# A convolution with a gated low-rank layer: the first five tiles in another order, and the router's query turned by VectorE

## What is computed

```python
out = conv1d(x, weight, groups=4, pad=4) + (c @ c_weight.T)[:, :, None] + bias[None, :, None]   # (32, 64, 1024)
q = einsum('bsd,rd->bsr', out, Wq_w)                  # router query, 16 numbers a row
scores = einsum('bsr,er->bse', q, keys)               # 64 experts
gate = softmax over the 16 best scores, 0 elsewhere
z = einsum('bsd,nd->bsn', out, A_w)                   # 512 = 64 experts x 8
y = einsum('bsn,on->bso', z * gate per expert, B_w) * 2.0
result = x + y                                        # fp32
```

## Time and profile before

| | |
|---|---|
| median of 3 runs | 237.67 us (236.91 to 238.66) |
| profiled execution, own time | 237.78 us |
| span in the profile | 235.8 us |
| granted TensorE clock, mean | 1.0 |
| TensorE busy | 231.0 us of the span |
| VectorE busy | 179.2 us |
| ScalarE busy | 98.3 us |
| HBM traffic | 161 GB/s over the span |

### The profile page before, as it was taken

The page is one execution under the profiler, slowest core; times in us unless marked ns, Lnnn a source line. Parts: engine busy times, 40 slices in busy tenths (PEclk is TensorE's granted clock), DMA queues, the critical chain, the costliest instruction groups (busy, mean ns, idle before and its releaser), DMA issues.

```text
span 235.8 us, 3992 instructions
## 1 busy us (share of the span) xinstructions
PE 231.0 (98%) x1398; PEld 206.4 (88%) x1398; DVE 179.2 (76%) x421; ACT 98.3 (42%) x245; POOL 1.6 (1%) x9
## 2 busy tenths in 40 slices
PE   8999999899999999999999999999999999999995
PEld 8988998598988989898898989889898988989884
DVE  1797799999969697996979698796969865644522
ACT  3897866255353253525424352532426241202100
POOL 2000000000000000000000000000000000000000
PEclk9999999999999999999999999999999999999999
DMA  6999017384644628263462816347282432616222
GB/s 196 379 403 379 10 47 224 100 276 161 177 152 100 244 70 258 77 186 147 105 235 71 276 58 194 138 105 234 72 240 93 121 146 51 220 45 222 92 89 89
DMA packets 22915, 38.22 MB, mean 162 GB/s; under 512 B 2544, under 2 KB 11120, under 8 KB 22896
## 3 DMA queue, kind: packets, MB, share of 16 engines
q1 hardware_dynamic: 22752, 37.89, 49.4%
q10 hardware_dynamic: 144, 0.08, 0.2%
HBM read 25.64 MB, written 12.32 MB: 161 GB/s over the span
## 4 chain that ended last, share of the span: by engine, by line
PE 93%; DVE 3%; issue 3%; ACT 0%; POOL 0%; DVEq 0%; POOLq 0%
PE p_z L608 36%; PE p_out L652 12%; PE p_out L653 12%; PE p_out L660 12%; PE p_conv L564 10%; PE p_conv L516 4%; PE p_out L608 3%; PE p_t L669 2%; PE p_out L516 1%; PE p_t L673 1%; DVE z_g L848 1%; PE p_t L622 1%; DVE h_lo L726 0%; DVE h_t L771 0%; DVE zt_lo L726 0%
## 5 line engine op out<-in xcount | busy, mean ns | idle before, releaser
L652 PE MATMUL p_out<-b_hi,zt_hi 128*128 128x512 f32 (+1 forms) x128 | 50.2, 393 | 0.0
L653 PE MATMUL p_out<-b_hi,zt_lo 128*128 128x512 f32 (+1 forms) x128 | 50.1, 393 | 0.0
L608 PE MATMUL p_z<-a_hi,h_hi 128*128 128x264 f32 x240 | 34.1, 285 | 1.0 <-DVE z_g L848 1.0
L608 PE MATMUL p_z<-a_lo,h_hi 128*128 128x264 f32 x240 | 35.0, 289 | 0.0
L660 PE MATMUL p_out<-b_lo,zt_hi 128*128 128x512 f32 (+1 forms) x128 | 34.5, 392 | 0.0
L608 PEld LDWEIGHTS p_z<-a_hi,h_hi 128*128 128x128 f32 x240 | 32.0, 188 | 2.6 <-issue 1.4
L608 PE MATMUL p_z<-a_hi,h_lo 128*128 128x264 f32 x240 | 34.2, 285 | 0.0
L608 PEld LDWEIGHTS p_z<-a_hi,h_lo 128*128 128x128 f32 x240 | 31.3, 188 | 0.0
L608 PEld LDWEIGHTS p_z<-a_lo,h_hi 128*128 128x128 f32 x240 | 31.0, 188 | 0.0
L343 ACT ACTIVATE h_hi<-h_t 128x1024 fp32r<-128x1024 f32 x16 | 17.0, 1064 | 31.5 <-DVE h_t L771 31.5
L726 DVE TENSOR_TENSOR x_lo<-x_blk,x_hi 128x1536 fp32r<-128x1536 f32 (+4 forms) x18 | 25.5, 1419 | 6.1 <-ACT x_hi L343 5.9
(11 more groups left out here) (100 smaller groups left out, 259.1 us busy)
## 6 DMA issues: line engine op xcount, KB each, us to landing
x_nat<-in_x_rows SPq DMA_DIRECT2D x16, 512.0 KB, 5.0
out_dram<-x_nat SPq DMA_DIRECT2D x31, 256.0 KB, 2.8
x_blk<-in_x_blocks SPq DMA_DIRECT2D x14, 516.0 KB, 4.4
z_dram<-a_raw SPq DMA_DIRECT2D x60, 64.0 KB, 1.8
a_raw<-z_dram SPq DMA_DIRECT2D x15, 256.0 KB, 3.8
a_raw<-in_a_wq SPq DMA_DIRECT2D x8, 264.0 KB, 6.3
x_nat<-in_b_w SPq DMA_DIRECT2D x4, 512.0 KB, 9.2
x_blk<-in_x_blocks SPq DMA_DIRECT2D x2, 258.0 KB, 3.9
```

The source lines that it names most:

```text
L608: mm = nc.tensor.matmul(z_bank(t, b)[:, 0:HB], h[:, t % 2, r, :], a[:, r, b * HB:(b + 1) * HB], start=k == 0 and r == 0, stop=k == 2 and r ...
L652: nc.tensor.matmul(dst, zt_hi[:, t % 2, c, :], b_hi[:, c, cols], start=c == 0, stop=False)
L653: nc.tensor.matmul(dst, zt_lo[:, t % 2, c, :], b_hi[:, c, cols], start=False, stop=False)
```

## The change

In the steady loop, from tile 5 on (TS = 5), TensorE no longer turns the query. ScalarE writes it twice side by side into `q_s` (128 rows by 32), VectorE turns it in four blocks of 32 by 32 into the diagonal blocks of `q_d`, ScalarE rounds that to `q_hi`, and one VectorE instruction makes `q_t`: its rows hold the high part and, under a mask column, the low part. The keys get a second set of 64 columns, so `scores` has 128 columns, and a sum over the two halves takes the place of the copy of the scores. TensorE's body becomes: z of tile i, the three shared products of the convolution of tile i+2 (`conv_sum`), `scores(i)`, the other six (`conv_pair`), and the second product. Tiles 3 and 4 take the way of tiles 0 to 2.

In the beginning, one of the eight products of ones goes, `cw` and the products for `u` are made in two halves (`products_u(0)` ahead of `conv_first`, `products_u(1)` behind its first four matmuls), and the lists of ScalarE and VectorE are in another order. On SP's queue, `z_in(1)` moves ahead of `load_rows(1)`. `small` grows from 164 to 229 columns.

```diff
 TW = 5
-TS = 3
+TS = 5
 NN = 8
...
-        q_s = sb("q_s", [P, P], F32R)
+        q_w = sb("q_w", [P, P])
+        q_s = sb("q_s", [P, 2 * RD])
+        q_d = sb("q_d", [P, P])
+        q_hi = sb("q_hi", [P, P], F32R)
         q_f = sb("q_f", [P, P])
         q_t = sb("q_t", [P, P], F32R)
-        k_r = sb("k_r", [P, E], F32R)
+        k_r = sb("k_r", [P, 2 * E], F32R)
+        k_hi = sb("k_hi", [P, E], F32R)
         sc = sb("sc", [P, E])
...
             z_out(1)
+            z_in(1)
             load_rows(1)
-            z_in(1)
             load_rows(2)
...
             nc.gpsimd.memset(ident[:], 0.0).then_inc(s_iz, 1)
-            nc.gpsimd.memset(q_s[:].bitcast(F32), 0.0).then_inc(s_qz, 1)
+            nc.gpsimd.memset(q_w[:], 0.0).then_inc(s_qz, 1)
+            nc.gpsimd.memset(q_d[:], 0.0).then_inc(s_qdz, 1)
             pool.wait_ge(s_iz, 1)
...
                                     pattern=[[-1, P]], channel_multiplier=1).then_inc(s_ident, 1)
-            pool.wait_ge(s_small, 16)
-            nc.gpsimd.tensor_copy(cw[:], sm[:, SMALL_CW:SMALL_CW + 64].rearrange("d (g c) -> d g c", c=CI).unsqueeze(2)
-                                  .to_broadcast([P, NG, R, CI])).then_inc(s_cw, 1)
+            pool.wait_ge(s_cw, 1)
+            nc.gpsimd.tensor_copy(cw[:, 2:NG], sm[:, SMALL_CW + 2 * CI:SMALL_CW + NG * CI].rearrange("d (g c) -> d g c", c=CI)
+                                  .unsqueeze(2).to_broadcast([P, NG - 2, R, CI])).then_inc(s_cw, 1)
...
                 act.wait_ge(s_cs, t - TW + 1)
+                if t == 2 * TG:
+                    act.wait_ge(s_u, 2)
                 if t > TW:
...
                     act.wait_ge(s_qz, 1)
-                if i >= 1:
+                if 1 <= i < TS:
                     act.wait_ge(s_qtp, i)
+                if i > TS:
+                    act.wait_ge(s_qd, i - TS)
                 query = z_bank(i, 1)[:, J - HB:HB]
                 if i < TS:
-                    high(q_s[:, 0:RD].bitcast(F32), query, s_q)
+                    high(q_w[:, 0:RD], query, s_q)
                 else:
-                    high(q_s[:, 0:4 * RD].rearrange("p (k d) -> p k d", d=2 * RD)[:, :, 0:RD],
-                         query.unsqueeze(1).to_broadcast([P, 2, RD]), s_q)
+                    high(q_s[:].rearrange("t (k d) -> t k d", k=2), query.unsqueeze(1).to_broadcast([P, 2, RD]), s_q)
...
                 act.wait_ge(s_qtp, i + 1)
-                high(q_f[:] if i < TS else q_t[:], p_t[:, 0:P], s_qt)
+                high(q_f[:], p_t[:, 0:P], s_qt)
+            def split_q(i):
+                act.wait_ge(s_qd, i - TS + 1)
+                high(q_hi[:], q_d[:], s_qhi)
...
                 act.wait_ge(s_small, 16)
-                high(k_r[:], sm[:, SMALL_K:SMALL_K + E], s_khi)
+                high(k_r[:, 0:E], sm[:, SMALL_K:SMALL_K + E], s_khi)
+                high(k_hi[:], sm[:, SMALL_KH:SMALL_KH + E], s_khi)
...
             take_q(0)
+            split_h(1)
             copy_q(0)
-            split_h(1)
             add_u(3)
-            split_x(4)
-            split_w(1)
             exp(0)
             split_h(2)
+            split_x(4)
+            take_q(1)
+            split_w(1)
+            copy_q(1)
             split_b(0)
             split_b(1)
-            take_q(1)
-            copy_q(1)
+            take_q(2)
+            exp(1)
+            copy_q(2)
+            split_h(3)
+            split_z(0)
             split_b(2)
-            exp(1)
-            take_q(2)
-            split_h(3)
-            copy_q(2)
             split_b(3)
-            split_z(0)
             add_u(4)
+            exp(2)
             sum_w(1)
-            exp(2)
             split_x(5)
             take_q(3)
+            split_z(1)
             split_h(4)
-            split_z(1)
             for i in range(3, NT):
...
                     take_q(i)
-                copy_q(i)
+                if i < TS:
+                    copy_q(i)
+                else:
+                    split_q(i)
                 if i > 3:
...
+            def products_u(pair):
+                pe.wait_ge(s_cw, pair + 1)
+                for g in (2 * pair, 2 * pair + 1):
+                    mm = nc.tensor.matmul(u_bank(pair)[:, g % 2 * P:g % 2 * P + SMALL_KH - SMALL_C], cw[:, g].rearrange("d r c -> d (r c)"),
+                                          sm[:, SMALL_C:SMALL_KH], start=True, stop=True)
+                mm.then_inc(s_up, 1)
...
                     direct(0, 0, ab, 0, True, False)
+                products_u(1)
                 pe.wait_ge(*x_lo_done(0, 0))
...
-            def conv_shared(t):
+            def conv_sum(t):
                 g = t // TG
...
+            def conv_pair(t):
+                g = t // TG
                 for ab in range(2):
...
             def conv(t):
-                if t >= TW:
-                    conv_shared(t)
-                else:
-                    conv_direct(t, (0, 2, 1))
+                conv_direct(t, (0, 2, 1))
...
                         pe.wait_ge(s_hhi, t + 1)
+                        if t == 0:
+                            pe.wait_ge(s_u, 2)
                         if t == 1:
...
                 pe.wait_ge(s_q, i + 1)
-                if i >= TS:
-                    pe.wait_ge(s_qlo, i - TS + 1)
                 if i == 0:
...
                     pe.wait_ge(s_qt, i)
-                nc.tensor.transpose(p_t[:, 0:P], q_s[:].bitcast(F32), ident[:]).then_inc(s_qtp, 1)
+                nc.tensor.transpose(p_t[:, 0:P], q_w[:], ident[:]).then_inc(s_qtp, 1)
...
             def scores(i):
-                pe.wait_ge(s_qt, i + 1)
+                if i < TS:
+                    pe.wait_ge(s_qt, i + 1)
+                else:
+                    pe.wait_ge(s_qlo, i - TS + 1)
                 if i == TS:
...
             pe.wait_ge(s_ones, 1)
-            for _ in range(8):
+            for _ in range(7):
                 nc.tensor.matmul(p_t[:, 0:P], ones[:], ones[:], start=True, stop=True)
-            pe.wait_ge(s_cw, 1)
-            for g in range(NG):
-                mm = nc.tensor.matmul(p_t[:, g * P:g * P + SMALL - SMALL_C],
-                                      cw[:, g].rearrange("d r c -> d (r c)"),
-                                      sm[:, SMALL_C:SMALL], start=True, stop=True)
-            mm.then_inc(s_up, 1)
+            products_u(0)
             conv_first()
...
                 z_product(i, 1, (0,), range(R))
-                turn_q(i)
+                if i < TS:
+                    turn_q(i)
                 z_product(i, 2, (0,), range(R))
+                if i + 2 < NT:
+                    conv_sum(i + 2)
                 scores(i)
                 if i + 2 < NT:
-                    conv(i + 2)
+                    conv_pair(i + 2)
                 out_part(i - 2, 0)
...
             def split_keys():
-                dve.wait_ge(s_khi, 1)
-                low(k_r[2 * RD:3 * RD], sm[2 * RD:3 * RD, SMALL_K:SMALL_K + E], k_r[2 * RD:3 * RD], s_klo)
+                dve.wait_ge(s_khi, 2)
+                low(k_r[:, E:2 * E], sm[:, SMALL_KH:SMALL_KH + E], k_hi[:], s_klo)
+            def turn_q(i):
+                dve.wait_ge(s_q, i + 1)
+                if i == TS:
+                    dve.wait_ge(s_qdz, 1)
+                for b in range(4):
+                    block = slice(32 * b, 32 * b + 32)
+                    last = nc.vector.transpose(q_d[block, block], q_s[block, :])
+                last.then_inc(s_qd, 1)
             def split_q(i):
-                dve.wait_ge(s_q, i + 1)
-                low(q_s[:, RD:2 * RD], z_bank(i, 1)[:, J - HB:HB], q_s[:, 0:RD], s_qlo)
+                dve.wait_ge(s_qhi, i - TS + 1)
+                dve.wait_ge(s_scp, i)
+                nc.vector.scalar_tensor_tensor(out=q_t[:], in0=q_hi[:].bitcast(F32), scalar=sm[:, SMALL_M:SMALL_M + 1],
+                                               in1=q_d[:], op0=ALU.mult, op1=ALU.add).then_inc(s_qlo, 1)
...
                 dve.wait_ge(s_scp, i + 1)
-                nc.vector.tensor_copy(sc[:], scores_at(i)).then_inc(s_dve, 1)
+                scored = scores_at(i)
+                if i < TS:
+                    nc.vector.tensor_copy(sc[:], scored).then_inc(s_dve, 1)
+                else:
+                    nc.vector.tensor_reduce(sc[:], scored.rearrange("t (k e) -> t e k", k=2), axis=mybir.AxisListType.X,
+                                            op=ALU.add).then_inc(s_dve, 1)
...
+            def add_bias(pair):
+                gs = slice(2 * pair, 2 * pair + 2)
+                dve.wait_ge(s_up, pair + 1)
+                nc.vector.tensor_tensor(u[:, gs], u_bank(pair)[:, 0:2 * P].rearrange("c (g n) -> c g n", n=P)[:, :, 0:32],
+                                        sm[:, SMALL_B + 2 * pair:SMALL_B + 2 * pair + 2].unsqueeze(2).to_broadcast([P, 2, 32]),
+                                        ALU.add).then_inc(s_u, 1)
+            dve.wait_ge(s_small, 16)
```

(60 more changed lines are left out.)

## The result

The changed kernel runs in 235.5 us (median of 6, 235.1 to 235.88) against 238.06 for the kernel before on the same chip: 0.9912 of it, interval 0.9886 to 0.9938. In a second set it was 235.26 against 237.6: 0.9903, interval 0.9875 to 0.9931. The forecast was 235.4.

The account below looks back on a forecast made before the run. TensorE's own list was taken to bound the kernel, with VectorE setting the time in the beginning. From the profiled 237.78 us, -1.29 (beginning), -1.32 (turn) and +0.22 (fp32 scores) gave 235.39, forecast 235.4, range 234.7 to 237.0.

Parts of the forecast that it names:

- The beginning: Tiles 0 to 4: VectorE's list between the copy for tile 1 and tile 2's gate shrinks, tile 3 starts earlier, -1.29 us.
- The pause for the exponential: VectorE's wait before tile 2's weighing: 0.44 us saved, since exp(2) now stands ahead of sum_w(1) on ScalarE.
- My ceiling of 1.55: Start of tile 3: TensorE's own work would allow 45.05 us, so at most 1.55 us could be gained.
- The turn: TensorE's list, tiles 5 to 15: the query's turn leaves it, 0.12 us a tile, -1.32 over eleven tiles.
- keep their price: Scores among TensorE's convolution products: 0.11 us for 64 columns and for 128, bounded by a weight load.
- The price of 56 to 81 ns: Lower price per turn from the skill: 0.6 to 0.9 us for eleven turns, a time of 235.9 to 236.1.
- fp32 scores: Tiles 3 and 4 on TensorE: two instructions for one, 0.11 us more each, +0.22.
- The first 20 us: Start of the kernel, one product of ones less and u's products moved: next to nothing, 0 to -0.1 us, not counted.
- The new wait: scores(i) waits for VectorE's split_q: 2.3 us of work fits in 3.18, 0.8 left, about 0.1 in tile 14.
- the deciding point: VectorE's query blocks: from 0.40 us a block the new way exceeds its cover; each further 0.1 costs 0.4 a tile.
- Rival (D): Slower: the query's new way is longer than its cover; 239.8 us at 0.5 us a block; chance 0.08.
- VectorE's load: Steady tiles: VectorE's work grows by 1.1 us a tile, first MAX8 0.28 later, the gate's wait stays covered.

Follow-up runs that it names:

- the doses: Changed kernel with each of the four query blocks turned twice, the first time into an unread tile: 238.35 us; with two of the four turned twice: 235.7 us.

## Why the prediction was right

**The forecast** of 235.4 stands against 235.5 and 235.26, and both parts exist on their own. Its two gains were each a little too large: by its own sum the profiled execution should have taken 235.39, and it took 235.88. The late input block explains 0.22 and the two sizes below 0.40; that is 0.13 more than the 0.49, and the time outside the span was 1.8 us where it was 2.0 before. The closeness is in part luck. The traces hold 1.15 + 1.06 - 0.23 = 1.98 us of gain and not 2.39, and the medians, which the forecast was set against, fell by 2.34 and 2.56.

**The beginning**, -1.29 in the sum, measured -1.15. The mechanism was right: VectorE's list between the copy for tile 1 and the gate of tile 2. The list shrank by 12.78 - 11.59 = 1.19 for 1.28. The copy itself comes 0.04 later from `split_x(2)` on. `split_w(1)` now fills VectorE directly ahead of it, and it starts 0.04 behind the end of TensorE's scores (32.70 + 0.33), as it did before (0.03): both are ready together, and which holds it isn't shown. The pause for the exponential was worth 0.46 for my 0.44. My ceiling of 1.55 was too high. In the kernel before, the last eight products ahead of tile 3 are these, with a wait in them for VectorE's `b_lo`:

```profile
43.43 2.21 PE L660 MATMUL p_out<-b_lo,zt_hi 128*128 128x512 f32 x8
```

At 0.233 each they would have ended in time for a start at 45.29, not 45.05, so no more than 1.3 could come of it.

**The turn**, -1.32, measured -1.06. The 0.12 a turn is right: 48 products of z take 5.84 us now and took 5.96 with the turn in them (120.25 - 114.41 and 121.37 - 115.41). Two things take from it. The scores don't quite keep their price among the convolution products: they and nine products take 2.20 or 2.21 now (122.45 - 120.25) and took 2.19 before (123.56 - 121.37), and the period says 0.02 in all, 0.2 over nine tiles. With 64 columns it is no different, so it isn't the width; why it is so stays open. And tile 14 gained 0.05 only, because there the scores' weights wait for `q_t`: the second product behind comes after 0.40 for 0.34. The price of 56 to 81 ns from the Trainium skill ("TensorE: Matmul & The Clock Gate", section "Back-to-back issue gap") is under what a turn cost here, 0.12. (The time that the prediction gives by it should begin at 235.8 and not 235.9.)

**fp32 scores**, +0.22, measured 0.11 + 0.12.

**The first 20 us**, nothing: shown by the kernels with and without the new start.

**The new wait.** Blocks of 0.2 us not overlapped, 0.85 for my 0.8; `split_q` 0.35 for 0.3. From the end of `q_t` to the product of the scores it is 0.80 us in a steady tile (133.79 to 134.59), which is my 0.8. But the wait is at the load of the weights, which stands 0.23 ahead of the product, and that step I left out. To the load it is 0.43 to 0.57, of which 0.05 is hand-over, and in tile 14 nothing is left of my 0.1: the load waits there. I put the deciding point at 0.40 us a block. The present 0.85 for four plus the 0.64 of the doses is 1.49, so 0.37. Rival (D) is real: with every block turned twice, 1.71 in all or 0.43 a block, the kernel was slower than before. By the prediction's point of 0.40 that costs 4 * 0.03 = 0.11 a tile, and it cost 0.22. The 0.36 that I expected ahead of that run was too high, because it counted the load's delay and not the product's.

**VectorE's load**, +1.1 a tile, measured 1.2. The first MAX8 comes 0.30 later in the tile for my 0.28 (121.64 - 114.18 against 122.34 - 115.18), and the gate still ends 2 us ahead of its use.

**Left open.** The kernel before spreads over 236.49 to 239.17 us in 27 runs, the changed one over 235.03 to 235.53 in 6. The landing of the inputs moves `split_x(2)` between 9.88 and 11.10 in the thirteen profiles, which is 1.2 us and not 2.7, and no profile was taken of the slow end. So the medians hold 0.4 to 0.6 us (2.34 and 2.56 against 1.98) that the traces don't account for.

## What to carry to other kernels

Where one engine is busy at 98%, look for the few stretches in which its waits still are: there the order of another engine's list decides, and one exchanged line can be worth 0.46 us. A step can leave the bound engine for one with slack if its new way is shorter than the cover that stands ahead of its use. Count that cover to the weight load and not to the product, and look at a distance of 0.05 us between an operand's end and the load with suspicion: here it was a wait, even where the profile prints none. Measure the slack by doses: up to it a dose is free, beyond it it costs. When comparing profiles of two kernels, anchor them at the first instruction behind the input transfers, or the landing of a block is taken for an effect.

## What was not expected of the hardware

The granted clock reads 1.00, the level of 2.4 GHz, in the first 7.2 us of every profile. Yet in the profile of the kernel before TensorE's fp32 products of ones stand about 0.23 us apart at the top, and its first convolution products of 256 columns 0.22 us and then, from 7.3 us on, 0.12. The moment isn't fixed: with the same start and only new lists, the first convolution products stood 0.13 us apart from 5.35 us on. A small matmul costs TensorE about 0.11 us between large ones whether it has 64 or 128 columns.
